# Making the first message table of a four-layer graph network inside the third gather pass

## The chip, the cores and the metric

One core of a Trainium2 chip runs the whole program. The metric is the time of one execution on the device in microseconds. TensorE (PE), VectorE (DVE), ScalarE (ACT), GpSimd (POOL) and SyncE (SP) each run their own instruction list in order and meet at semaphores. All work is in float32.

## What is computed

Four graph layers follow each other over 12,500 nodes of 128 features and 200,000 edges, sorted by destination. The edges stay the same; each layer gathers source rows and sums them by destination. The end of the third layer and the start of the fourth are what matters here:

```
x  = layernorm(x + sage2(relu(sage1(x))))        # third layer, two weighted gathers
h  = x                                            # fourth layer, three steps
for _ in range(3):
    t   = einsum('nd,kod->kno', h, W_et) + b_et   # a row per node and edge type (4 types)
    msg = t[etypes, src]
    a   = segment_sum(msg, dst)
    h   = gru(a, h)
gate = sigmoid(concat([h, x]) @ i_w.T + i_b)
out  = layernorm(x + gate * (h @ j_w.T + j_b))
```

The table `t` of the first step, 12,500 rows of 4 x 128 numbers, must be complete in HBM before the fourth layer's first gather can start.

## The kernel before, in words

Nodes are handled in 25 groups of 512 (`GN`, four tiles `A` of 128). There are six gather passes: pass 1 is the second layer, passes 2 and 3 are the two halves of the third, passes 4 to 6 are the steps of the fourth. A pass walks over 71 turns of four quarters q. In a quarter

- ScalarE copies the source indices of four slots into `stage` (line 1214), once TensorE has summed the same quarter of the turn before (semaphore `summed`), and counts `staged`;
- GpSimd waits for `staged` and issues four indirect DMAs (line 1012), 128 rows each, into `ring`;
- VectorE adds the sum of the turn before to `acc` (line 2007) and builds four one-hot matrices (line 2044, `hot_ready`);
- TensorE, when the rows have landed and the one-hots are there, sums the four slots (line 1566).

Beside that the most used source and destination pairs are summed as dense blocks. SyncE loads them as units from `t_pairs` into two halves of a buffer (lines 652 and 657), VectorE reduces a unit over the types (line 2032) and TensorE multiplies it (line 1549). There are six units in a **step** of two turns. The sixth is left unreduced in passes 2 and 3: TensorE multiplies it straight from the buffer, four matmuls of 128x512 at the end of the step (line 1544), and SyncE may load the second unit of the next step, which takes the same half of the buffer, only after `dense_done` has counted these four.

`pairs_of_turns` (line 448) writes this order out: `body(p)` is the even turn 2p and then the odd turn 2p+1, for p from 0 to 33. Into the quarters of body p the work on one finished group, step p-1, is laid as `parts`. In pass 3, TensorE transposes the group's rows in quarter 0 of the even turn (line 1604) and multiplies in quarter 1 (lines 1625, 1626). ScalarE copies sums and rows in quarter 0 of the odd turn (lines 1248, 1252) and takes the root in quarter 2 (line 1258), for which it waits on VectorE's moments (line 2167). VectorE combines and takes the moments in quarter 1 of the odd turn (lines 2202 to 2167) and writes the normed rows in quarter 3 (line 2179, `step_rows`), which SyncE stores to `t_x` (line 724). There are 33 such steps in the loop, some of them on a dummy group, and three in the tail of the pass: 36 for 25 groups.

After pass 3 there is a stage of its own for the table. For each of the 25 groups SyncE reads the rows back (line 743), TensorE transposes them (line 1364), ScalarE makes two copies, one of them the state `aux` (lines 1267, 1269), TensorE multiplies by the types' weights (line 1640), VectorE adds the bias (line 2233) and SyncE stores (line 738). GpSimd's first gather of pass 4 waits for the last store.

Of the kernel before, what the change touches and what calls it, by code (L numbers as in the profile page):

```python
# [14 lines left out]
P = 128  # L15
# [67 lines left out]
def build(nc, x, src, dst, edge_attr_32, edge_type_4, edge_weight, L0_gnn_W, L0_gnn_b, L1_gnn_u, L1_gnn_W1,  # L83
# [4 lines left out]
    with ctx:  # L88
# [15 lines left out]
        X3 = dram("t_x3", [ROWS, D])  # L104
        TT = [dram(f"t_types{i}", [ROWS, KT * D]) for i in range(2)]
# [78 lines left out]
        t_slot = ring.rearrange("p s f -> p (s f)").rearrange("p (s f) -> p s f", s=4)  # L184
# [10 lines left out]
        dense_sum = work[:, 9 * GN:12 * GN].rearrange("p (s f) -> p s f", s=TILES)  # L195
        own = [work[:, (12 + i) * GN:(13 + i) * GN] for i in range(5)]
# [134 lines left out]
        class Dense:  # L331


            def __init__(self, name, loads, prod=True, norm=True, out_=True):
# [8 lines left out]
                if prod and name != "tt":  # L343
                    self.prod = sem(f"{name}_prod")
                if prod and name not in ("wx", "tt"):
                    self.free = sem(f"{name}_free")
# [22 lines left out]
        p_t = Dense("tt", 0, norm=False, out_=False)  # L369
        p_gate = Dense("value", 1, norm=False, out_=False)  # L370
        p_fin = Dense("fin", 1, prod=False)
        state_rows = [sem(f"state_rows{i}") for i in range(2)]
# [8 lines left out]
        t_prod = [sem(f"t_prod{i}") for i in range(2)]  # L381
        t_rows = [sem(f"t_rows{i}") for i in range(2)]
        t_out = [sem(f"t_out{i}") for i in range(4)]
# [81 lines left out]
        def all_steps(eng):  # L465

            eng.wait_ge(regs_ready, 2)
            return loaded(eng.engine, step_total[0:1, 0:1], 1, STEPS + NG, "the kernel writes one of two numbers",
                          STEPS + TAIL_STEPS)[0]

# [49 lines left out]
        def _(sp):  # L520
# [212 lines left out]
            def t_store(at):  # L733

                for hh in range(2):
                    slot = 2 * at.par + hh
                    sp.wait_ge(t_rows[hh], at.g + 1)
                    sp.dma_start(rows(TT[0], at.g)[:, hh * 2:hh * 2 + 2, :], by_tile(t_slot[:, slot, :], 2)
                                 ).then_inc(t_out[slot], 16)


            def state_in(at):
                sp.dma_start(by_tile(cand[:, at.par, :]), rows(X3, at.g)).then_inc(state_rows[at.par], 16)
            state_in(At(0, 0))

            def t_step(at):
                if not at.last:
                    wait(sp, p_t.turned, at.g)
                    state_in(at.plus(1))
                if not at.first:  # L750
                    t_store(at.plus(-1))
            groups(sp, t_step)
            t_store(LAST)

            for slot in range(4):
                sp.wait_ge(t_out[slot], 16 * (NG // 2 + 1 - slot // 2))
# [36 lines left out]
        def _(pool):  # L793
# [237 lines left out]
            for n in range(3):  # L1031
                if n == 0:
                    for slot in range(4):
                        go(t_out[slot], 16 * (NG // 2 + 1 - slot // 2))
# [8 lines left out]
        def _(act):  # L1043
# [165 lines left out]
            def stage_pass(ph, index, k, parts):  # L1209

                def turn(t, part=None):
                    for q in range(NQ):
                        wait(act, summed, (ph - 1) * PS + last(t, q))
                        act.activation(stage[:, q * K:q * K + K], cols(index, t * U + q * K, K), ACT.Copy).then_inc(staged, 1)  # L1214
                        if part is not None and q in parts:
                            part(q)

                def body(p, units):
                    first = isinstance(p, int) and p == 0
                    turn(p * 2)  # L1220
                    g = None if first else step_of(mybir.EngineType.Activation, p - 1)
                    turn(p * 2 + 1, None if first else lambda q: parts[q](before(total, k, p - 1), g, done_by(ph, p - 1, False), before(total, min(k, 1), p - 1)))
                pairs_of_turns(act, body)
                turn(SURE - 1)
# [8 lines left out]
                def step(m):  # L1233
                    g = step_of(mybir.EngineType.Activation, m)
                    for q in sorted(parts):
                        parts[q](before(total, k, m), g, done_by(ph, m, True), before(total, min(k, 1), m))
# [6 lines left out]
            def rows_turned(features=False):  # L1243

                def part(i, g, done, normed_):
# [9 lines left out]
            def step_root():  # L1255
                def part(i, g, done, normed_):
# [7 lines left out]
            stage_pass(3, meta_src, 2, {0: rows_turned(), 2: step_root()})  # L1264
            def state_step(at):
                act.wait_ge(p_t.turned, at.g + 1)
                act.activation(cols(aux, at.g * GN, GN), bank[at.par][:, :], ACT.Copy)
                wait(act, t_prod[1], at.g - 1)
                act.activation(auxs[:, at.par, :], bank[at.par][:, :], ACT.Copy).then_inc(p_t.copied, 1)
            groups(act, state_step)  # L1270


            def gates(i, g, done, normed_):
# [6 lines left out]
            def new_state(i, g, done, normed_):  # L1280
# [38 lines left out]
        def _(pe):  # L1319
# [23 lines left out]
            def ahead(d, prod, slot=None):  # L1343

                turn_rows(d, At(0, 0), slot)

                def step(at):
                    if not at.last:
                        wait(pe, d.copied, at.g)
                        turn_rows(d, at.plus(1), slot)  # L1350
# [4 lines left out]
            def turn_rows(d, at, slot=None):  # L1355

                if slot is None:
                    d.wait_rows(pe, at)
                    src_ = xin[:, at.i, :]
                else:  # L1360
                    pe.wait_ge(state_rows[at.par], (at.pair + 1) * 16)
                    src_ = slot[:, at.par, :]
                for a in range(A):
                    mm = pe.transpose(bank[at.par][:, a * P:(a + 1) * P], src_[:, a * D:(a + 1) * D], ident[:, :])
# [164 lines left out]
            def gather_pass(ph, k, parts, features=False):  # L1529
# [22 lines left out]
                def turn(t, block=None, part=None):  # L1552
                    for q in range(NQ):
# [16 lines left out]
                        if part is not None and q in parts:  # L1570
                            part(q)

                def body(p, units):
# [6 lines left out]
                    turn(p * 2, block, None if first else  # L1580
                         lambda q: parts[q](before(total, k, p - 1), g, done_by(ph, p - 1, False), before(total, min(k, 1), p - 1)))
                    turn(p * 2 + 1, lambda i: block(TILES + i))
# [9 lines left out]
                def step(m):  # L1592
                    g = step_of(mybir.EngineType.PE, m)
                    for q in sorted(parts):
                        parts[q](before(total, k, m), g, done_by(ph, m, True), before(total, min(k, 1), m))
                tail_steps(pe, total, step)

            def turn_step(per):

                def part(i, g, done, normed_):  # L1600
                    pe.wait_ge(step_in, (i + 1) * 16 if per == 1 else normed_ * 32 + 32)
                    wait(pe, step_free, i)
                    for a in range(A):
# [4 lines left out]
            def l1_prod(i, g, done, normed_):  # L1608
# [11 lines left out]
            def l2_prod(wl, wr):  # L1620

                def part(i, g, done, normed_):
                    pe.wait_ge(step_copied, i + 1)
                    for a in range(A):
# [8 lines left out]
            gather_pass(3, 2, {0: turn_step(2), 1: l2_prod(W_2L, W_2R)})  # L1633

            def types(at):

                for a in range(A):
                    if a % 2 == 0:
                        wait(pe, t_rows[a // 2], at.g)
                    mm = pe.matmul(bank[2 + a][:, :], auxs[:, at.par, a * P:(a + 1) * P],  # L1640
                                   wT[:, W_ET:W_ET + KT, :].rearrange("p k f -> p (k f)"), start=True, stop=True)
                    if a % 2:
                        mm.then_inc(t_prod[a // 2], 1)
            ahead(p_t, types, slot=cand)

            def gate_sums(i, g, done, normed_):
# [675 lines left out]
```

## Time and profile before

| | us |
|---|---|
| median of three runs (15437.32 to 15471.95) | 15470.18 |
| the profiled execution | 15606.01 |
| its span | 15604.3 |
| gathers of pass 3 | 7995 to 9831 |
| tail of pass 3 | 9831 to 9888 |
| the table's own stage | 9888 to 10027 |
| passes 4, 5, 6 | 10027, 11850, 13670 onwards |

The profiled execution is 136 us slower than the median of the runs. Over the span TensorE is busy 64%, GpSimd 62%, VectorE 44%, ScalarE 9%. These are averages over stages with different limits, so they say little about one of them: a stage is to be read by its own rows and by what ends its waits.

### The profile page before, as it was taken

The page shows a single profiled execution, that of the slowest core. Times are in us where ns is not written, and L with a number is a line of the kernel's source. Part 1 is how long each engine was busy: PE and PEld are TensorE (multiplying, and loading weights), DVE is VectorE, ACT ScalarE, POOL GpSimd, SP SyncE. Part 2 cuts the span into 40 slices and gives each one's busy share as a digit, 9 for nine tenths or more (in the row PEclk, how much of TensorE's full clock was granted, in tenths as well). Part 3 has the DMA queues.
Part 4 walks back from the last instruction along what each step waited for, and adds up shares of the span by engine and source line. Part 5 has one row for each costly group of instructions (what it writes and reads, how often), then busy time and mean ns, then how long its engine had stood idle before and what let it go on. Part 6 is the DMA issues. An engine that isn't in the chain of part 4 may idle for free. (4 is left out here: it accounts for less than half of the span.)

```text
span 15604.3 us, 173214 instructions
## 1 busy us (share of the span) xinstructions
PE 10001.7 (64%) x37130; PEld 6386.2 (41%) x37131; DVE 6791.8 (44%) x20397; ACT 1405.0 (9%) x4108; POOL 9688.3 (62%) x8863
## 2 busy tenths in 40 slices
PE   5777774444466666555545555587876888677775
PEld 3444444334344444333333333344443444334443
DVE  3333333333466764666646665333332333222223
ACT  1111111111100000000000000100000000000001
POOL 3888887777646665666655555366664666566662
PEclk6555656667777886667766676799987999788886
DMA  8888887777787774777746666577764777467773
GB/s 271 196 197 197 196 173 152 165 161 122 127 209 189 189 187 117 188 187 189 190 123 175 180 180 164 155 212 203 210 187 137 211 210 208 128 183 190 192 190 84
DMA packets 4070001, 2778.79 MB, mean 178 GB/s; under 512 B 430093, under 2 KB 3820298, under 8 KB 4069630
## 3 DMA queue, kind: packets, MB, share of 16 engines
q1 hardware_dynamic: 3529604, 2147.73, 50.0%
q0 software_dynamic: 508368, 612.97, 20.7%
q10 hardware_dynamic: 31722, 15.04, 0.3%
q14 instruction: 241, 1.97, 0.0%
q8 instruction: 66, 1.08, 0.0%
HBM read 2025.54 MB, written 778.19 MB: 180 GB/s over the span
## 5 line engine op out<-in xcount | busy, mean ns | idle before, releaser
L1012 POOL DMA_INDIRECT ring<-t_types,stage x3408 | 3263.5, 958 | 2275.8 <-issue 1405.0
L1012 POOL DMA_INDIRECT ring<-t_x,stage x2272 | 2207.4, 972 | 1524.4 <-issue 896.7
L1544 PE MATMUL bank<-work 128*128 128x512 f32 x5216 | 2645.9, 652 | 635.1 <-DMA work<-t_types 259.9
L1566 PE MATMUL bank<-ring 128*128 128x128 f32 x13632 | 2285.4, 323 | 1021.1 <-DVE ring L2044 323.9
L1566 PEld LDWEIGHTS bank<-ring 128*128 128x128 f32 x13632 | 2124.4, 232 | 1825.6 <-issue 1574.2
L2032 DVE TENSOR_REDUCE work<-work 128x512 f32<-128x2048 f32 x524 | 1912.1, 3649 | 823.0 <-DMA work<-t_pairs 749.2
L968 POOL DMA_INDIRECT t_sums<-ring,stage x1136 | 1765.3, 1554 | 443.5 <-issue 256.0
L2007 DVE TENSOR_TENSOR acc<-acc,bank 128x128 f32 x1704 | 480.0, 282 | 3513.6 <-remote 2056.2
L1544 PEld LDWEIGHTS bank<-work 128*128 128x128 f32 x5216 | 1041.3, 211 | 1782.5 <-issue 1439.5
L1012 POOL DMA_INDIRECT ring<-t_h,stage x1136 | 1077.7, 949 | 812.9 <-ACT stage L1214 424.7
L1549 PE MATMUL bank<-work 128*128 128x512 f32 x1048 | 734.3, 789 | 547.3 <-issue 320.7
L2044 DVE TENSOR_SCALAR ring<-iota_f,meta_low 128x128 f32<-128x128 f32 x4544 | 999.3, 289 | 1.7 <-issue 1.4
L1443 PE MATMUL bank<-aux 128*128 128x128 f32 x2272 | 527.7, 407 | 571.1 <-ACT aux L1141 535.8
L987 POOL DMA_INDIRECT t_pairs<-acc,pair_stage x432 | 675.6, 1564 | 332.8 <-DMA t_pairs<-acc,pair_stage 192.2
L1910 DVE SCALAR_TENSOR_TENSOR aux<-bank,aux,upto 128x128 f32<-128x128 f32 x1136 | 330.6, 347 | 1182.5 <-PE bank L1428 853.8
L1503 PE MATMUL bank<-aux 128*128 128x128 f32 x864 | 221.4, 437 | 930.5 <-ACT aux L1181 930.5
L1562 PE MATMUL bank<-ring,rec 128*33 128x128 f32 x2272 | 388.4, 324 | 613.3 <-issue 299.7
L1443 PEld LDWEIGHTS bank<-aux 128*128 128x128 f32 x2272 | 468.1, 305 | 704.7 <-ACT aux L1141 597.5
L994 POOL DMA_INDIRECT t_sums<-ring,stage x432 | 672.3, 1556 | 131.6 <-issue 129.5
L2044 DVE TENSOR_SCALAR ring<-iota_f,meta_low,meta_w 128x128 f32<-128x128 f32 x2272 | 653.4, 356 | 147.5 <-issue 145.9
L1562 PEld LDWEIGHTS bank<-ring,rec 128*33 128x33 f32 x2272 | 272.4, 132 | 808.3 <-issue 725.5
L1503 PEld LDWEIGHTS bank<-aux 128*128 128x128 f32 x864 | 189.8, 324 | 959.2 <-ACT aux L1181 958.6
(298 smaller groups left out, 11218.8 us busy)
## 6 DMA issues: line engine op xcount, KB each, us to landing
work<-t_pairs SPq DMA_DIRECT2D x2352, 512.0 KB
t_pairs<-acc SPq DMA_DIRECT2D x272, 740.0 KB
t_pairs<-acc SPq DMA_DIRECT2D x272, 370.0 KB
t_pairs<-acc SPq DMA_DIRECT2D x74, 1360.0 KB
work<-t_types SPq DMA_DIRECT2D x294, 256.0 KB
t_types<-work SPq DMA_DIRECT2D x144, 512.0 KB
ring<-t_types,stage POOLq DMA_INDIRECT x3408
ring<-t_x,stage POOLq DMA_INDIRECT x2272
```

The source lines that it names most:

```text
L968: pool.indirect_dma_start(TAB[k], bass.IndirectOffsetOnAxis(ap=stage[:, u:u + 1], axis=0), msg[:, u, :], None, compute_op=ALU.add).then_in ...
L987: pool.indirect_dma_start(rows_, bass.IndirectOffsetOnAxis(ap=pair_stage[:, u:u + 1], axis=0), pair_out[:, b, k * 2 * P:(k + 1) * 2 * P], ...
L994: pool.indirect_dma_start(TAB[k], bass.IndirectOffsetOnAxis(ap=stage[:, u:u + 1], axis=0), msg[:, u, :], None, compute_op=ALU.add).then_in ...
L1012: pool.indirect_dma_start(msg[:, u, :], None, table, bass.IndirectOffsetOnAxis(ap=stage[:, u:u + 1], axis=0)).then_inc(slot_dma[u], 16)
L1443: mm = pe.matmul(bank[4 + q][:, k * P:(k + 1) * P], dups[:, q, k * P:(k + 1) * P], wx_rows[:, q, :], start=True, stop=True)
L1544: mm = pe.matmul(bank[4 + half][:, :], dense_t[:, tile, k_ * D:(k_ + 1) * D] if ph > 3 else dense_x[:, tile, :], dense_b[:, half, k_ * 4:( ...
L1549: mm = pe.matmul(bank[4 + half][:, :], dense_x[:, tile, :], dense_sum[:, c % TILES, :], start=first, stop=end)
L1562: pe.matmul(bank[q][0:DE + 1, P:2 * P], rec[:, u, 0:DE + 1], hot[:, u, :], start=k_ == 0, stop=k_ == K - 1)
L1566: mm = pe.matmul(bank[q][:, 0:P], msg[:, u, :], hot[:, u, :], start=k_ == 0, stop=k_ == K - 1)
L2007: v.tensor_tensor(into, into, bank[q][:, 0:P], ALU.add).then_inc(added, 1)
L2032: v.tensor_reduce(dense_sum[:, c % TILES, :], dense_b[:, half, :, :].rearrange("p (k b) c -> p (b c) k", k=KT), AXIS.X, ALU.add).then_inc( ...
L2044: ins = v.tensor_scalar(hot[:, q * K + k_, :], iota_f[:, :], low(c + k_), weight(c + k_) if weight else None, ALU.is_equal, ALU.mult if we ...
```

## The change

The stage for the table disappears. Its work is laid into pass 3 as `heads`, per step, 36 times, with the normed rows taken from the tile `s_res` where they were read back from HBM.

- TensorE, in the odd turn of body p, after its sum in the quarter (and after the dense unit): quarter 0 transposes the rows of step p-1, for which it waits on `step_rows`; quarters 1 and 2 each make two tiles of the table, each tile as a one-row matmul that puts the bias in and a 128x512 matmul; quarter 3 makes another product, with the gate's weights.
- ScalarE, in the even turn of body p+1, after its index copies of quarters 1, 2 and 3: the two copies of the transposed rows; tiles 0 and 1; tiles 2 and 3 and then the gate product. Each of these is a wait for TensorE, a wait for the DMA that last left this slot, a copy of 128x512 and a DMA issued on ScalarE's own queue.
- Two slots: `rec` for tiles 0, 2 and the gate product, `b2_all` for tiles 1 and 3.
- A new tensor `t_gate` in HBM takes the gate product; no instruction reads it.
- New waits: TensorE's transposes of the next step and its next products wait for ScalarE's copies (`head_rows`); the norm waits for the transposes of the step before (`head_turned`).
- `pairs_of_turns` writes three bodies out ahead of its loop, before it was two.

```
-            body(0, NH * TILES)
-            body(1, NH * TILES)
-            with turns(eng, 2, LEAD) as p:
+            for p in range(3):
+                body(p, NH * TILES)
+            with turns(eng, 3, LEAD) as p:
...
+            def head_turn(i, m):
+                pe.wait_ge(step_rows, i + 1)
+                for a in range(A):
+                    mm = pe.transpose(bank[6][:, a * P:(a + 1) * P], s_res[:, a * D:(a + 1) * D], ident[:, :])
+                mm.then_inc(head_turned, 1)
+            def head_types(two):
+                def part(i, m):
+                    if two:
+                        pe.wait_ge(head_rows, m * 5 + two)
+                    else:
+                        pe.wait_ge(head_copied, m + 1)
+                    for a in (two, two + 1):
+                        pe.matmul(bank[7 - a % 2][:, :], ones_f[0:1, :], bet_all[0:1, :], start=True, stop=False)
+                        pe.matmul(bank[7 - a % 2][:, :], s_xT[:, a * P:(a + 1) * P],
+                                  wT[:, W_ET:W_ET + KT, :].rearrange("p k f -> p (k f)"), start=False, stop=True).then_inc(head_prod, 1)
+                return part
+            def head_gate(i, m):
+                pe.wait_ge(head_rows, m * 5 + 3)
+                for a in range(A):
+                    mm = pe.matmul(bank[7][:, a * D:(a + 1) * D], s_xT[:, a * P:(a + 1) * P], wT[:, W_I + 1, :], start=True, stop=True)
+                mm.then_inc(head_prod, 1)
+            gather_pass(3, 2, {0: turn_step(2), 1: l2_prod(W_2L, W_2R)},
+                        heads={0: head_turn, 1: head_types(0), 2: head_types(2), 3: head_gate})
...
+            def head_keep(m, a, slot, into):
+                act.wait_ge(head_prod, m * 5 + (a + 1))
+                wait(act, head_out[slot], m * HEAD_OUTS[slot] + a // 2 * 16)
+                act.activation(head_slots[slot], bank[7 - slot][:, :], ACT.Copy).then_inc(head_rows, 1)
+                act.wait_ge(head_rows, m * 5 + (a + 1))
+                act.dma_start(into, by_tile(head_slots[slot], A if a == A else 1)).then_inc(head_out[slot], 16)
...
-            groups(sp, t_step)
-            t_store(LAST)
-            groups(act, state_step)
-            ahead(p_t, types, slot=cand)
-            groups(v, t_add)
```

## Rows read from the trace of the kernel before

**Rows 1.** Windows: pass 3, the table's stage, pass 5, pass 6; columns in its head.

```profile
core 0: us, PE busy (x) PEld busy (x) DVE busy (x) ACT busy (x) POOL busy (x), PEclk, DMA share, GB/s
7995.00:9831.00 1836.00, 936.04 (x3508) 642.51 (x3508) 1125.45 (x2203) 95.37 (x379) 1076.80 (x1136) 0.69 0.65 170
...
9887.80:10027.50 139.70, 105.44 (x300) 47.99 (x300) 68.23 (x118) 27.41 (x54) 0.04 (x1) 0.93 0.74 247
11850.00:13600.00 1750.00, 1363.58 (x4508) 733.62 (x4508) 523.61 (x1743) 117.13 (x380) 1084.61 (x1136) 0.89 0.71 194
13670.00:15370.00 1700.00, 1282.93 (x4228) 698.13 (x4228) 437.03 (x1600) 114.39 (x379) 1089.25 (x1135) 0.86 0.68 179
```

**Rows 2.** Waits in pass 3: who waited for whom, us in total, times, longest.

```profile
POOL ring L1012 <- ACT stage L1214: 424.7, 69, 9.2
...
ACT std L1258 <- DVE mv L2167: 453.1, 33, 16.8
```

**Rows 3.** Timeline of one step of pass 3: start, duration, instruction, [idle before <- releaser].

```profile
9013.84 3.65 DVE L2032 TENSOR_REDUCE work<-work 128x512 f32<-128x2048 f32 x1 [14.87 <-DMA work<-t_pairs]
...
9023.84 3.55 PE L1566 MATMUL bank<-ring 128*128 128x128 f32 x16 [0.40 <-issue]
...
9032.34 0.30 ACT L1258 ACTIVATE std<-mv,eps_col 128x4 f32<-128x4 f32 x1 [15.30 <-DVE mv L2167]
...
9033.54 0.95 POOL L1012 DMA_INDIRECT ring<-t_h,stage  x1 [8.50 <-ACT stage L1214]
...
9038.63 1.11 DVE L2179 TENSOR_SCALAR work<-work,mv,rstd 128x128 f32<-128x128 f32 x4
...
9044.16 5.27 PE L1544 MATMUL bank<-work 128*128 128x512 f32 x8
...
9057.39 0.94 POOL L1012 DMA_INDIRECT ring<-t_h,stage  x1 [0.30 <-issue]
...
9059.79 4.24 SPq L652 DMA_DIRECT2D work<-t_pairs  x4
...
9062.11 0.20 ACT L1214 ACTIVATE stage<-meta_src 128x4 uint32 x1 [17.41 <-remote]
...
9066.01 3.66 DVE L2032 TENSOR_REDUCE work<-work 128x512 f32<-128x2048 f32 x1 [15.62 <-DMA work<-t_pairs]
```

**Rows 4.** Timeline of pass 2: two of its 32 steps, line 1544 and SyncE's next load.

```profile
6680.94 4.17 PE L1544 MATMUL bank<-work 128*128 128x512 f32 x8
...
6699.83 1.00 SPq L652 DMA_DIRECT2D work<-t_pairs  x2
...
7643.79 4.03 PE L1544 MATMUL bank<-work 128*128 128x512 f32 x8
...
7647.68 0.70 SPq L652 DMA_DIRECT2D work<-t_pairs  x1
```

**Rows 5.** Prices by line (min/median/max ns): a one-row matmul, a copy, a DMA issue, landing of 738.

```profile
L1377 PE MATMUL bank<-work,ones_f x50: 587/1056/1217, 70.3 to 241.9; 1*128 1x512 f32 x50
...
L1252 ACT ACTIVATE work<-bank x33: 578/579/580, 8065.1 to 9740.5; 128x512 f32<-128x512 f32 x33
...
L1105 ACTq DMA_DIRECT2D t_wx<-work x25: 378/397/7279, 75.4 to 244.3; - x25
...
DMA to landing us min/median/max: 2.8/3.0/4.7
```

**Rows 6.** Timeline of pass 3's tail, the table's stage and the start of pass 4.

```profile
9870.63 1.11 DVE L2179 TENSOR_SCALAR work<-work,mv,rstd 128x128 f32<-128x128 f32 x4
...
9872.41 1.12 PE L1604 MATMUL bank<-ident,work 128*128 128x128 f32 x4 [6.74 <-DMA work<-t_x]
...
9883.55 1.11 DVE L2179 TENSOR_SCALAR work<-work,mv,rstd 128x128 f32<-128x128 f32 x4
...
10009.54 7.03 PE L1640 MATMUL bank<-wT,work 128*128 128x512 f32 x16
...
10027.46 0.94 POOL L1012 DMA_INDIRECT ring<-t_types,stage  x1 [195.53 <-issue]
```

More of the change, by code:

```diff
@@ L368, in build @@
         gate_link = sem("gate_link")
-        p_t = Dense("tt", 0, norm=False, out_=False)
+        head_turned, head_copied, head_prod, head_rows = (sem(f"head_{n}") for n in ("turned", "copied", "prod", "rows"))
+        head_out = [sem(f"head_out{i}") for i in range(2)]
         p_gate = Dense("value", 1, norm=False, out_=False)
         p_fin = Dense("fin", 1, prod=False)
-        state_rows = [sem(f"state_rows{i}") for i in range(2)]
         gate_prod = sem("gate_prod")
@@ L731, in _ @@
             layer_pass(3, 2, [(s_xin, H1), (s_yin, X2)], H1, X3)
[L733 to L751, printed above, removed]
-            groups(sp, t_step)
-            t_store(LAST)
-            for slot in range(4):
-                sp.wait_ge(t_out[slot], 16 * (NG // 2 + 1 - slot // 2))
+            for slot in range(2):
+                sp.wait_ge(head_out[slot], total * HEAD_OUTS[slot])
             def state_pass(n):
@@ L1032, in _ @@
                 if n == 0:
-                    for slot in range(4):
-                        go(t_out[slot], 16 * (NG // 2 + 1 - slot // 2))
+                    for slot in range(2):
+                        go(head_out[slot], total * HEAD_OUTS[slot])
                 else:
@@ L1207, in _, with stage_pass, turn @@
             total = all_steps(act)
-            def stage_pass(ph, index, k, parts):
-                def turn(t, part=None):
+            def stage_pass(ph, index, k, parts, heads=()):
+                def turn(t, part=None, ahead=None):
                     for q in range(NQ):
@@ L1216, in turn, with head @@
                             part(q)
+                        if ahead is not None and q:
+                            for i in (q - 1,) if q < NQ - 1 else (q - 1, q):
+                                ahead(i)
+                def head(m):
+                    if not heads:
+                        return None
+                    g = step_of(mybir.EngineType.Activation, m)
+                    return lambda q: heads[q](m, g) if q in heads else None
                 def body(p, units):
                     first = isinstance(p, int) and p == 0
-                    turn(p * 2)
+                    turn(p * 2, None, None if isinstance(p, int) and p < 2 else head(p - 2))
                     g = None if first else step_of(mybir.EngineType.Activation, p - 1)
-                    turn(p * 2 + 1, None if first else lambda q: parts[q](before(total, k, p - 1), g, done_by(ph, p - 1, False), before(total, min(k, 1), p - 1)))
+                    turn(p * 2 + 1, None if first else lambda q: parts[q](before(total, k, p - 1), g, done_by(ph, p - 1, False), before(total, min(k, 1), p - 1), p - 1))
                 pairs_of_turns(act, body)
-                turn(SURE - 1)
+                turn(SURE - 1, None, head(STEPS - 1))
                 used = used_turns(mybir.EngineType.Activation)
@@ L1235, in step @@
                     for q in sorted(parts):
[L1236 removed]
+                        parts[q](before(total, k, m), g, done_by(ph, m, True), before(total, min(k, 1), m), m)
+                    for q in sorted(heads):
+                        heads[q](m, g)
                 tail_steps(act, total, step)
@@ L1341, in spread, with ahead @@
                 return mm
-            def ahead(d, prod, slot=None):
-                turn_rows(d, At(0, 0), slot)
+            def ahead(d, prod):
+                turn_rows(d, At(0, 0))
                 def step(at):
@@ L1569, in turn @@
                             block(q - 1)
-                        if part is not None and q in parts:
+                        if part is not None and q in at:
                             part(q)
```

124 lines of the change are left out of this document (58 added, 66 removed).

## The prediction, made before the changed kernel was run

> **What bounds the kernel now.** I read the windows first, to see the price of the stage that goes. The table's stage takes 139.7 us with TensorE busy for 105 of them and no gather under way [rows 1]. That is the most the change can win outside pass 3: 0.9% of the span. So what decides is what pass 3 pays for the work it takes in.
>
> Averages leave room there: in 1836 us TensorE is busy for 936, GpSimd for 1077, ScalarE for 95 [rows 1]. The waits correct this. GpSimd stood 424.7 us for ScalarE's index copies and ScalarE 453.1 us for VectorE's moments, 33 times [rows 2]. So I followed one step through its timeline [rows 3]; all 32 steps of the loop look alike. It is a closed ring:
>
> - VectorE starts on the second dense unit at 9013.84 and works without a pause to the end of the norm at 9038.63 + 1.11 = 9039.74: **25.9 us**.
> - Its moments release ScalarE's root at 9032.34, behind which the next index copy is queued; gathers resume at 9033.54, land, are summed, and line 1544 starts at 9044.16: **4.4 us** after the norm's end.
> - SyncE may load the next step's second unit only after line 1544. By its record that ends at 9049.43, but SyncE issues at 9059.79: **15.6 us** from the start of line 1544.
> - The load lets VectorE start at 9066.01: **6.2 us**.
>
> 25.9 + 4.4 + 15.6 + 6.2 = 52.1; from 9013.84 to 9066.01 it is 52.2. This ring, not an engine's busy share, is the bound of pass 3.
>
> **What is removed.** The stage: 142.8 us from the last norm's end (9884.66) to the first gather of pass 4 at 10027.46 [rows 6]. SyncE's 25 reads and VectorE's 100 adds go with it; they cost nothing beyond it.
>
> **What remains at the end.** Each of the three tail steps gets its head behind its norm, in series: transposes 1.1, two copies 1.2, four tiles at two 128x512 matmuls each (0.88 each by line 1640, eight in 7.03 us [rows 6]; 1.06 by the median of the one-row matmul [rows 5]) with a copy of 0.6 between halves, some 8.5, then the gate product's copy, which waits for the landing of tile 2's DMA because both leave from the same slot: 3.0 [rows 5]. About 15 us to the last copy, then 0.4 to issue and 3.0 to land. Before, the next step's transposes began 0.7 us after a norm (9871.74 to 9872.41 [rows 6]); ScalarE will now be some 12 us later, twice: 24. With 17 to 18 for the last head and some 6 from the last landing to a first gather, 48 remain of 142.8. **The end wins 95 us** (bounds 85 to 103: all matmuls at the low or the high clock).
>
> **What is added to a step of pass 3, 32 times.** TensorE gets four transposes, eight 128x512 matmuls (four of them one row deep, which cost the same [rows 5]) and four small ones: 9 us at the high clock, 17 at the low one. The busy share would carry that. The place is the trouble. Transposing step p-1 stands in quarter 0 of the odd turn and waits for the norm, which VectorE writes in quarter 3 of the same turn. The sums of quarters 0 and 1 now run at 9023.84 to 9027.39 and the norm ends at 9039.74 [rows 3], with VectorE busy all the way. So TensorE stands for about 15 us after its first sum, and everything behind it in its list comes after the norm: transposes 1.1, sum 1.8 (3.55 for two [rows 3]), unit 1.1, two tiles 5.3 (four matmuls, as line 1544 takes here [rows 3]), sum 1.8, unit 1.1, two tiles 5.3, sum 1.8, and only then line 1544. That is 19.3 us where 4.4 stand now; at the high clock 12.7, at the low one 24. ScalarE's copies between the halves lie beside the units. I take **17**, since the granted clock is 0.69 in this pass and 0.89 in pass 5, where TensorE has more to do [rows 1].
>
> Against that, the 15.6 us behind line 1544 can shrink. They aren't matmul time. In pass 2 the same four matmuls release SyncE 3.9 us after their start in one step (7643.79 to 7647.68) and 18.9 in another (6680.94 to 6699.83) [rows 4]. Where it is long, the release comes shortly after GpSimd's last gather (1.5 us after 9058.33 [rows 3]); the trace doesn't say why. Bounds 3.9 and 18.9; with GpSimd running dry earlier in the new step I take **10**, between.
>
> The Trainium skill (Perfetto Trace Analysis, Tensor Engine Instruction) says that a matmul's end in a trace is estimated and that its semaphore moves when PSUM has acknowledged the writes. By that alone the release would follow the records at about 5 us, and the sum below would be 54.1 a step, and in all 34 us faster than now; the trace disagrees here in every step (15.6).
>
> ScalarE gets seven copies of 0.58 and five issues of 0.4 a step [rows 5]: 6 us, in pieces behind index copies; the gate's piece waits 3 us or more for a landing and comes ahead of the odd turn's first index copy. TensorE's line 1544 covers it; without that cover it costs 3 to 5 us a step. VectorE gets nothing; its new wait is long satisfied. SyncE's queue loses nothing in the pass. DMA gets 1.25 MB a step where 8.9 go through now (170 GB/s for 52 us): nothing to 1 us in landing.
>
> **The sum.** 25.9 + 17 + 10 + 6.2 = 59.1 a step against 52.2: 6.9 more, 32 times, 221 us. Less 95 at the end: **126 us slower** than the profiled 15606, 15732. The runs' median lies 136 lower; put on it, 15470 + 125 gives 15595. The break-even is 3.0 us a step: the two uncertain terms (17 and 10) together must stay under 23.
>
> **The rivals.**
>
> - *The ring stays near its length, and the stage's time is won (faster).* Place: between line 1544 and SyncE's load. If the 10 fall to 3.9, the step is 53.0, 0.8 more: 26 less 95, 69 us faster, 15400. With TensorE at the high clock throughout (12.7) it would be 48.7 and 15265. For it: the short release in pass 2 [rows 4], and the clock of 0.89 in pass 5 [rows 1]. It decides from a release under 6 us at 17. Against it: 15.6 in every step of this very pass.
> - *They cancel*: 17 and a release of 5 to 7: 15430 to 15510.
> - *The release stays at 15.6* and the chain is 19.3: 67.0 a step, 14.8 more, 474 less 95: 15850. For it: the release is that long now [rows 3]. The Trainium skill (TensorE: Matmul & The Clock Gate, The HAM clock gate) says that an idle array falls to the half clock and gets the full one back only with sustained work. A stand of 15 us just ahead of the chain would then put it at 19 to 24 and not at 13.
> - *ScalarE's piece with the gate product comes late* by 3 to 5 us in each step: 100 to 160 on top of the forecast, 15700 to 15750.
> - *The change doesn't do what it says*: 36 heads are made for 25 groups and a gate table that nobody reads is stored. That is counted above.
>
> **The numbers.** Forecast, a step longer by 4.5 to 12 us: 0.5. Release and chain at their long ends, or ScalarE late beyond that: 0.12. Cancelled: 0.15. Faster: 0.23. About 0.3% (46 us) is what a measurement of this kernel can tell from no change. So slower 0.62, same 0.15, faster 0.23. The range takes in the cases from most of the faster one to the release at 15.6: 15380 to 15860; the forecast's own is 15520 to 15760.
>
> **What would show it.** In pass 3, the transposes of the head must start right after line 2179's end, with an idle of 12 us or more before them put down to VectorE; line 1544 some 17 us after the norm; a step of 57 to 63 us; GpSimd's wait for ScalarE over 425 us. Pass 4 must start about 48 us after the last norm. I am wrong if TensorE doesn't stand for the norm, if the step stays at 52 or 53 with a release under 6 us, or if passes 4 to 6 change by more than a few us.

## The result, and the profile after

The changed kernel takes **15,703 us** (median of 4 runs, 15,679 to 15,713) where the kernel before takes 15,471 (4 runs): a ratio of **1.0153, 95% interval 1.0137 to 1.0169**, 232 us slower. Forecast were 125 us more, with 0.62 for slower.

First gather to last gather, from the traces, in us:

| | pass 3 | last gather of pass 3 to first of pass 4 | both | the profiled execution |
|---|---|---|---|---|
| before | 1835.6 | 196.5 | 2032.1 | 15,606.0 |
| after | 2125.5 | 124.1 | 2249.6 | 15,703.6 |
| difference | +289.9 | -72.4 | **+217.5** | +97.6 |

The profiled execution of the kernel before stood 136 above its median; in that of the changed kernel every pass that the change doesn't touch is 19 to 27 us shorter, pass 5 for example 1704 against 1725. Set against the medians (+232), the +217.5 of the stretch that was changed is nearly the whole result.

The windows of the changed kernel (core 0): pass 3, the time from the last norm to the first gather of pass 4, and passes 5 and 6 (columns as in [rows 1]).

```profile
7943.00:10070.00 2127.00, 1342.15 (x4432) 765.91 (x4432) 1116.33 (x2202) 227.13 (x610) 1077.41 (x1136) 0.69 0.62 167
10163.10:10193.20 30.10, 18.98 (x28) 6.65 (x28) 14.67 (x19) 4.56 (x11) 0.00 (x0) 0.50 0.32 99
11989.00:13694.00 1705.00, 1361.22 (x4492) 730.58 (x4492) 521.96 (x1731) 116.62 (x379) 1089.69 (x1136) 0.90 0.72 199
13788.00:15468.00 1680.00, 1261.52 (x4228) 689.45 (x4228) 438.13 (x1599) 113.62 (x379) 1092.02 (x1136) 0.87 0.68 181
```

TensorE took in 406 us of work in pass 3 (936 before), and the pass grew by 290: 9.1 us in each of 32 steps. The granted clock stayed at 0.69.

The waits of pass 3 (who waited for whom: us in total, times, longest):

```profile
POOL ring L989 <- ACT stage L1191: 728.3, 155, 8.2
...
ACT std L1247 <- DVE mv L2195: 495.2, 33, 17.9
...
PE bank L1649 <- DVE work L2209: 451.7, 32, 14.8
...
ACT rec L1264 <- DMA t_types<-rec: 5.3, 3, 2.6
```

The third line is the new one: 32 times TensorE stood for the norm (line 2209 now), 14.1 us each. GpSimd's wait for indices rose from 425 [rows 2] to 728. The last line says that ScalarE hardly ever waited for a slot's landing.

One step of the changed kernel from its norm on, to be laid beside [rows 3]: line 2209 is the norm, 1649 the head's transposes, 1569 the sums, 1660 the one-row matmuls of the bias, 1661 the table's matmuls, 1547 the dense unit that SyncE's load (651) waits for.

```profile
9031.92 1.11 DVE L2209 TENSOR_SCALAR work<-work,mv,rstd 128x128 f32<-128x128 f32 x4 [0.22 <-DVE rstd L2202]
...
9033.08 1.11 PE L1649 MATMUL bank<-ident,work 128*128 128x128 f32 x4 [14.00 <-DVE work L2209]
...
9039.48 2.07 PE L1660 MATMUL bank<-bet_all,ones_f 1*128 1x512 f32 x2 [1.87 <-ACT work L1258]
...
9041.48 2.08 PE L1661 MATMUL bank<-wT,work 128*128 128x512 f32 x2
...
9047.36 1.91 PE L1569 MATMUL bank<-ring 128*128 128x128 f32 x8
...
9051.52 1.12 PE L1660 MATMUL bank<-bet_all,ones_f 1*128 1x512 f32 x2 [1.26 <-ACT b_all L1264]
...
9058.23 1.74 PE L1569 MATMUL bank<-ring 128*128 128x128 f32 x8
9059.80 3.60 PE L1547 MATMUL bank<-work 128*128 128x512 f32 x8
...
9063.43 4.28 SPq L651 DMA_DIRECT2D work<-t_pairs  x4
...
9069.86 3.65 DVE L2060 TENSOR_REDUCE work<-work 128x512 f32<-128x2048 f32 x1 [19.05 <-DMA work<-t_pairs]
```

The transposes start 0.05 us after the norm's end (9033.03). From there to line 1547 it is 26.8 us (4.4 before), of which the two halves of the table take 7.9 (9039.48 to 9047.36) and 6.7 (9051.52 to 9058.23). But SyncE is released **3.6 us** after line 1547 starts, where it was 15.6. From the release to VectorE it is 6.4 (6.2 before), and VectorE's part is 25.9, as before.

The granted clock of that chain, in three windows:

```profile
9033.00:9040.00 7.00, 5.05 (x15) 3.45 (x16) 3.10 (x12) 1.26 (x3) 3.67 (x4) 0.50 0.69 182
9040.00:9048.00 8.00, 8.00 (x12) 2.48 (x10) 3.13 (x1) 0.00 (x0) 2.98 (x4) 0.50 0.13 33
9048.00:9059.80 11.80, 10.54 (x24) 4.89 (x24) 1.31 (x5) 1.37 (x3) 3.79 (x4) 0.65 0.20 67
```

0.50 is the level of 1.2 GHz: the first half runs at it from end to end. This is not so in every step: in 17 of the 33 steps of the pass the first half takes 7.9 us, in the others 4.8 to 7.0.

The tail and the start of pass 4, beside [rows 6]:

```profile
10095.76 1.11 DVE L2209 TENSOR_SCALAR work<-work,mv,rstd 128x128 f32<-128x128 f32 x4 [0.21 <-DVE rstd L2202]
...
10129.20 1.11 DVE L2209 TENSOR_SCALAR work<-work,mv,rstd 128x128 f32<-128x128 f32 x4 [0.22 <-DVE rstd L2202]
...
10162.00 1.11 DVE L2209 TENSOR_SCALAR work<-work,mv,rstd 128x128 f32<-128x128 f32 x4 [0.22 <-DVE rstd L2202]
...
10193.32 0.94 POOL L989 DMA_INDIRECT ring<-t_types,stage  x1 [123.17 <-issue]
```

Two tail norms are 33.4 and 32.8 us apart where they were 12.9, and the first gather comes 30.2 us after the last norm's end.

### The profile page after: what moved, and what is told of

Its sections match the earlier page's. It is cut to its first block and busy times, and to the rows that moved or that the text cites. A ratio compares the mean times of both kernels' runs of the same rounds, so it can differ in the third digit from the quotient of the medians.

```text
span 15702.0 us, 174771 instructions
## 1 busy us (share of the span) xinstructions
PE 10338.2 (66%) x37838; PEld 6476.8 (41%) x37839; DVE 6714.4 (43%) x20297; ACT 1520.6 (10%) x4310; POOL 9701.8 (62%) x8863
## 5 line engine op out<-in xcount | busy, mean ns | idle before, releaser
L1547 PE MATMUL bank<-work 128*128 128x512 f32 x5216 | 2615.5, 646 | 586.6 <-DMA work<-t_types 227.1
L1552 PE MATMUL bank<-work 128*128 128x512 f32 x1048 | 721.3, 777 | 366.4 <-issue 240.6
L1446 PEld LDWEIGHTS bank<-aux 128*128 128x128 f32 x2272 | 475.2, 309 | 679.0 <-ACT aux L1118 599.6
L1191 ACT ACTIVATE stage<-meta_src 128x4 uint32 (+1 forms) x852 | 170.8, 203 | 4400.7 <-PE bank L1569 2069.9
```

Source lines behind the costliest of these rows:

```text
L1446: mm = pe.matmul(bank[4 + q][:, k * P:(k + 1) * P], dups[:, q, k * P:(k + 1) * P], wx_rows[:, q, :], start=True, stop=True)
L1547: mm = pe.matmul(bank[4 + half][:, :], dense_t[:, tile, k_ * D:(k_ + 1) * D] if ph > 3 else dense_x[:, tile, :], dense_b[:, half, k_ * 4:( ...
L1552: mm = pe.matmul(bank[4 + half][:, :], dense_x[:, tile, :], dense_sum[:, c % TILES, :], start=first, stop=end)
```

## The experiments

In all of them the kernel before takes **13,798 to 13,815 us**, not 15,471. They ran on three chips (which chip the first runs were on isn't recorded), and the three agree. So I took both kernels' profiles again beside the experiments. "This setting" below is that of these runs, "the first" that of the runs above. Each number below is set against the runs of the kernel before on the same chip; "step" is the median distance of line 1544 (or its successor) in pass 3.

**1. The bias left out** (so the first types' table lacks it): four of each head's eight 128x512 matmuls go.

```
-  pe.matmul(bank[7 - a % 2][:, :], ones_f[0:1, :], bet_all[0:1, :], start=True, stop=False)
   pe.matmul(bank[7 - a % 2][:, :], s_xT[...], wT[...],
-            start=False, stop=True)
+            start=True, stop=True)
```

> Leaves out the bias of the first types' table: the four one-row 128x512 matmuls of each head. Theory (the chain on TensorE from the norm's end to line 1547 sets the step): its two halves of four 128x512 matmuls took 8.0 and 6.9 us and shrink to about 4 each; the chain falls from 26 to 18 or 19 us, the release behind line 1547 stays at 3.9, the step falls from 62.1 to 54 or 55, 7 to 8 us 32 times; with 8 us less in each of three tail steps about 250 us less: 15455, bounds 15420 to 15510. Rival (chain and release share one bound, so that a shorter chain gives a longer release): chain 18, release 8 to 12, step 59 to 62: 15600 to 15690.

Measured: 13,924 us, 1.0092 (1.0075 to 1.0109) of the kernel before. Beside the changed kernel on these chips (14,232, experiment 6) that is 308 less: step 57.8 to 48.8, from the norm to line 1547 21.6 to 12.3, release 3.6. Forecast were 250. The chain theory stands, and nothing came back behind line 1547, though in this setting no kernel shows a long release (experiments 5 and 6). One step's second half:

```profile
8773.23 1.98 PE L1660 MATMUL bank<-wT,work 128*128 128x512 f32 x4 [1.40 <-ACT b_all L1264]
8775.05 1.05 PE L1569 MATMUL bank<-ring 128*128 128x128 f32 x8
8775.94 3.60 PE L1547 MATMUL bank<-work 128*128 128x512 f32 x8
```

Two matmuls in 1.8 us. In the changed kernel four take 6.3 (median): taking half of the work away removed more than two thirds of the time. What is left runs at the full clock: 1.00 in the second halves, where the changed kernel has 0.65.

**2. The gate product left out** (its table isn't read by anything): `heads={..., 3: head_gate}` goes on TensorE and ScalarE, and the counts of five pieces a head become four.

> Leaves out the gate product of each head, its copy and its store (a table that nobody reads). Theory (only what stands between the norm and line 1547 counts in the loop): the gate product stands behind line 1547, so the step stays at 62; only the tail gives back some 2 to 4 us a step: 15670 to 15700. Rival (ScalarE's gate piece comes ahead of the odd turn's first index copy and makes the gathers late by 3 to 5 us a step): 15540 to 15610.

Measured: 14,214 us, 1.0306 (1.0289 to 1.0323): 17 less than the changed kernel, most of it in the pass (8 us) and the tail (4). The rival with ScalarE's piece, 100 to 160 us in my prediction, falls.

**3. No wait for the norm.** The transposes read s_acc in place of s_res, so the table holds other values, and wait for the combining adds alone:

```
-  pe.wait_ge(step_rows, i + 1)
+  pe.wait_ge(step_free, i + 1)
-  ... pe.transpose(bank[6][...], s_res[...], ident[:, :])
+  ... pe.transpose(bank[6][...], s_acc[...], ident[:, :])
```

> The head's transposes read s_acc in place of s_res (the table's values are other ones), so TensorE waits in quarter 0 only for the combining adds (which end near 9030 in the step of rows 3) and not for the norm (9039.7); all the work stays. Theory (the stand for the norm is what lengthens the step): line 1547 comes about 26 us after the adds and not after the norm, some 9 us earlier; step 52 to 54: 15370 to 15460. Rival 1 (the work itself, at the low clock, costs it): step 60 to 62, 15640 to 15700. Rival 2 (the long release behind line 1547 comes back when TensorE is early): line 1547 earlier, release 12 to 16, step 59 to 62: 15600 to 15700.

Measured: 13,939 us, 1.0099 (1.0082 to 1.0116), so 293 less than the changed kernel with all of its work kept. TensorE still stood, for the adds:

```profile
PE bank L1649 <- DVEq L2249: 166.2, 32, 5.9
```

5.2 us each in place of 14. Line 1547 came some 13 us after the norm, step 49.6, release 4.2. The place of the wait, not the work, costs two thirds of the 434 us. Rival 2 (a long release coming back) can't be judged here, since no trace of this setting has one.

**4. The wait alone**, on the kernel before: nothing is moved, TensorE only waits for the norm in quarter 0.

```
-  turn(p * 2 + 1, lambda i: block(TILES + i))
+  turn(p * 2 + 1, lambda i: block(TILES + i), None if first or ph != 3 else
+       lambda q: pe.wait_ge(step_rows, before(total, k, p - 1) + 1) if q == 0 else None)
```

> The kernel before, with nothing moved, and one wait more: in pass 3 TensorE waits in quarter 0 of the odd turn for the norm of the step before, as the head's transposes do. Theory A (a stand of TensorE ends the long release behind line 1544): two units and three sums now follow the norm, line 1544 starts 8 to 9 us after it and not 4.4, the release falls from 15.6 to 4 or 5, the ring would be 45 and the step 45 to 50 us: 15220 to 15400. Theory B (the release is a thing of its own, or of GpSimd's stream, and stays near 15.6 or falls only by what the chain grew): step 52 to 56.5, 15470 to 15610.

Measured: 13,845 us, 1.0031 (1.0019 to 1.0044). One step:

```profile
8618.69 1.11 DVE L2180 TENSOR_SCALAR work<-work,mv,rstd 128x128 f32<-128x128 f32 x4
8620.15 2.04 PE L1566 MATMUL bank<-ring 128*128 128x128 f32 x8 [13.79 <-DVE work L2180]
...
8629.65 4.23 SPq L652 DMA_DIRECT2D work<-t_pairs  x4
```

(The norm is line 2180 in this kernel.) Line 1544 starts at 8626.02, 6.2 after the norm's end, and the release is 3.6. 25.9 + 7.2 + 3.6 + 6.5 = 43.2, and the step is 43.2: the ring adds up to the tenth. A stand of 14 us costs 45 us in all, when only three sums and two units are behind it. In pass 3 alone the wait costs 44 us (experiment 4), the work with a shorter wait 243 (experiment 3), and both together 509 (experiment 6): most of the price is that the work stands behind the wait. But neither theory on the release could be judged here, as the next two runs show.

**5 and 6. Both kernels again, unchanged.**

> The kernel before, unchanged, for its profile: the runs of the first four experiments, with the kernel before among them, took 13800 us where it took 15470 at first, and in their traces the release behind line 1544 or 1547 is 3.6 to 3.9 in pass 2 and 3 alike. Expected: the kernel before shows it too where it takes 13800: a release of about 3.6 in place of 15.6, and a step of pass 3 of 40 to 42 (25.9 + 4.4 + 3.6 + 6.5 = 40.4; 32 gathers at 1.25 are 40.0). Rival: its release stays near 15.6 and it is the changed kernels that lost it.

> The changed kernel, unchanged. If the chain alone sets the step where the release is short: 25.9 + 21 to 24 + 3.8 + 6.5 = 57 to 61 a step against 40 to 42 before, 18 us 32 times, less 70 to 90 at the end: 430 to 540 us slower than the kernel before on the same chip (14230 to 14340 where that takes 13800). Where the kernel before shows its long release: 230 us slower, as in the first runs. Rival: the change costs the same 230 us everywhere.

Measured: 13,804 us for the kernel before, and 14,232 for the changed one, 1.0316 (1.0299 to 1.0333): **434 us slower** than the 13,798 of all runs of the kernel before in that comparison. The two windows of the kernel before, passes 2 and 3:

```profile
5945.00:7366.00 1421.00, 859.97 (x3508) 589.93 (x3508) 1026.04 (x1773) 93.05 (x346) 1074.68 (x1135) 0.75 0.82 213
7422.00:8890.00 1468.00, 895.55 (x3508) 607.09 (x3508) 1114.83 (x2202) 98.07 (x379) 1079.82 (x1135) 0.71 0.82 212
```

1468 where [rows 1] have 1836, with the engines busy for nearly the same time (TensorE 896 for 936, GpSimd 1080 for 1077). Here is one release of it, line 1544 and SyncE, with GpSimd's gathers running on past it:

```profile
8551.08 4.41 PE L1544 MATMUL bank<-work 128*128 128x512 f32 x8
...
8555.53 4.12 SPq L652 DMA_DIRECT2D work<-t_pairs  x4
8555.86 0.94 POOL L1012 DMA_INDIRECT ring<-t_h,stage  x1 [0.30 <-issue]
```

4.4 us. Counted over all 32 steps of a pass, from the start of line 1544 or 1547 to SyncE's issue of the second unit's load, the one that waits for it:

| trace | pass 2: median, over 6 us | pass 3: median, over 6 us |
|---|---|---|
| before, first | 9.9, 31 of 32 | 15.9, 32 of 32 |
| after, first | 15.9, 31 of 32 | **3.9, 1 of 32** |
| before, again | 4.2, none | 4.6, none |
| after, again | 4.5, none | 3.8, none |

The short release of pass 2 in [rows 4] is not one. SyncE's issue at 7647.68 is the first unit's load (line 657, the rows that come with a first unit, follows it), and the second unit's came at 7653.23, 9.4 us after line 1544's start. The one short release of that pass is at 6344.45:

```profile
7647.68 4.92 SPq L652 DMA_DIRECT2D work<-t_pairs  x2
7652.70 0.35 SPq L657 DMA_DIRECT2D work<-t_x  x1
7653.23 7.83 SPq L652 DMA_DIRECT2D work<-t_pairs  x4
```

```profile
6344.45 3.60 PE L1544 MATMUL bank<-work 128*128 128x512 f32 x8
...
6348.08 8.82 SPq L652 DMA_DIRECT2D work<-t_pairs  x4
```

The long release belongs to the first runs, in both kernels, and no other trace has it. It is not line 1544's alone either. In [rows 3] ScalarE's index copy at 9062.11 comes as late: by its record the sum that it waits for had ended at 9050.32. Counted over the six passes of the kernel before, ScalarE was free and its index copy still came more than 5 us after the end of the sum that it waits for in 338 of 1680 cases in the first trace, at least 41 in each pass, and in none in the second. In the changed kernel's first trace it is 310, but 6 in pass 3. And all six passes of the kernel before are 269 to 367 us longer in its first trace than in its second.

In the changed kernel's first trace it is gone from pass 3, the one pass in which TensorE stands for the norm, and there in pass 2 of the same execution:

```profile
7071.01 4.64 PE L1547 MATMUL bank<-work 128*128 128x512 f32 x8
7087.80 4.10 SPq L651 DMA_DIRECT2D work<-t_pairs  x4
```

Where it doesn't exist, the change can't take it away, and costs 434 us in place of 232. The ring, median of its terms in pass 3:

| | VectorE | norm to 1544/1547 | release | landing | step |
|---|---|---|---|---|---|
| before, first | 25.9 | 4.2 | 15.9 | 6.2 | 52.3 |
| after, first | 25.9 | 25.0 | 3.9 | 6.4 | 62.1 |
| before, again | 25.9 | 4.3 | 4.6 | 6.5 | 41.4 |
| after, again | 26.0 | 21.6 | 3.8 | 6.6 | 57.8 |

Pass 3 is 1978 us for 1469, and from its last gather to the first of pass 4 it is 124.0 for 195.4: +509 - 71 = +437, the measured 434.

**7. The wait alone, a second time**, since it would tell the two theories apart where the long release occurs:

> The kernel before with the one wait more, a second time, for the case that the kernel before takes 15470 in these runs and not 13800: there the release behind line 1544 was 15.6 in pass 3 in every step, and 3.9 in pass 3 of the changed kernel, which is the only pass of that trace in which TensorE stands for VectorE. Theory A (the stand is what ends it): release 4 in pass 3 and 10 to 16 in the other passes, pass 3 about 250 us shorter than with the kernel before. Theory B (it is the amount of work on TensorE, or chance): 15 in pass 3 too. Where the kernel before takes 13800, as in the other runs: +45 us as before, release 3.6, and the question stays open.

Measured: 13,865 us, 1.0034 (1.0014 to 1.0054), release 3.6. The kernel before took 13,815 beside it: 50 us, as before, and the question stays open.

**8. Work in the stand.** Added to the changed kernel, with results that are overwritten:

```
+  pe.wait_ge(step_free, i + 1)
+  for a in range(5):
+      pe.matmul(bank[7][:, :], ident[:, :], wT[:, W_ET:W_ET + KT, :]..., start=True, stop=True)
   pe.wait_ge(step_rows, i + 1)
```

> The changed kernel with work added for the experiment: while TensorE stands for the norm it waits for the combining adds alone at first (they end some 9 us earlier) and then runs five 128x512 matmuls into bank 7, whose results are overwritten, before it waits for the norm. Theory (the stand puts TensorE to the low clock, and that makes the halves behind the norm cost 7 to 8 us each and not 5): the granted clock from the norm to line 1547 rises from 0.5 to 0.65 towards 1.0, the chain falls from 21.4 to 14 to 18 us, the step from 57.8 to 50 to 55: 90 to 240 us less than the changed kernel, 13990 to 14140 where that takes 14231. Rival (nine us of activity don't raise the clock, or the five matmuls overrun the norm by 1 to 3 us): chain 21 to 24, 14230 to 14320.

Measured: 14,225 us, 1.0302 (1.0285 to 1.0319), and step 58.0: no gain. Two windows of one step from the norm's end (8947.4) on, and two of the changed kernel's (8931.7) below them:

```profile
8947.40:8952.50 5.10, 4.52 (x19) 2.17 (x19) 3.32 (x11) 1.26 (x3) 3.88 (x5) 1.00 0.90 242
8952.50:8966.00 13.50, 12.10 (x23) 4.74 (x23) 4.27 (x6) 1.38 (x3) 6.42 (x7) 0.66 0.27 78
```

```profile
8931.70:8941.00 9.30, 9.30 (x23) 4.67 (x24) 6.31 (x11) 1.26 (x3) 6.57 (x7) 0.68 0.58 155
8941.00:8953.20 12.20, 11.10 (x28) 5.60 (x26) 1.32 (x5) 1.37 (x3) 3.79 (x4) 0.64 0.22 70
```

The five matmuls did what was hoped right behind the norm: the clock is 1.00, and the head's transposes, sum and unit took 3.0 us in place of 4.5 (medians). Then it fell, in the midst of the halves, and these took 5.0 and 6.9 in place of 4.8 and 6.3: the chain went from 21.6 to 20.9 and not to 14 to 18. The low stretch was moved, not removed, and my theory that the stand by itself makes the halves dear falls in that form.

**9. The heads behind line 1547** (without the gate product). The transposes go to quarter 3 of the odd turn, behind the dense unit; the halves to quarters 0 and 1 of the next even turn; the step's own transposes and product to quarters 2 and 3 of it. ScalarE's copies follow, and its root waits in quarter 3.

```
+  def both(q):                      # TensorE, even turn
+      if not (isinstance(p, int) and p < 2):
+          ahead_types(q, p)         # heads[q + 1] of step p - 2, for q < 2
+      if q > 1:
+          parts[q - 2](...)
+  turn(p * 2 + 1, ..., lambda q: heads[0](before(total, k, p - 1), p - 1), (NQ - 1,))
```

> The changed kernel without the gate product, and with its heads moved behind line 1547: the transposes in quarter 3 of the odd turn, the two halves in quarters 0 and 1 of the next even turn, the step's own transposes and product in quarters 2 and 3; ScalarE's copies follow, and its root waits in quarter 3 and not 2. Theory (the stand for the norm and the halves between norm and line 1547 cost the step): the transposes find the norm done, line 1547 comes 2 to 5 us after the norm; the step is 40 to 48 where the release is short (TensorE is then busy for 37 to 46 of it): -30 to +130 us against the kernel before; where the release is long, 50 to 54: -100 to +40. Rival (TensorE's 16 us of work itself is too much in a step): 55 to 60, as the changed kernel.

Measured: 13,683 us, **0.9915 (0.9899 to 0.9932), 114 us faster than the kernel before** and 548 faster than the changed kernel. One step, with the norm (2236), the dense unit (1560) and the head (1676, 1687, 1688):

```profile
8421.72 1.11 DVE L2236 TENSOR_SCALAR work<-work,mv,rstd 128x128 f32<-128x128 f32 x4 [0.24 <-DVE rstd L2229]
...
8424.13 3.60 PE L1560 MATMUL bank<-work 128*128 128x512 f32 x8
...
8427.57 0.60 PE L1676 MATMUL bank<-ident,work 128*128 128x128 f32 x4
8427.76 4.51 SPq L651 DMA_DIRECT2D work<-t_pairs  x4
...
8429.43 1.12 PE L1687 MATMUL bank<-bet_all,ones_f 1*128 1x512 f32 x2 [0.37 <-ACT work L1271]
...
8430.48 1.12 PE L1688 MATMUL bank<-wT,work 128*128 128x512 f32 x2
...
8434.76 1.13 PE L1582 MATMUL bank<-ring 128*128 128x128 f32 x8 [1.05 <-DMA ring<-t_h,stage]
```

The transposes wait for nothing, line 1560 comes 1.3 us after the norm (median 1.1), and the first half takes 4.3 us (8429.43 to 8433.72). The pass is 1433 us, and 1136 gathers at 1.25 us, their distance where GpSimd waits for nothing, need 1420: GpSimd's gathers nearly fill it now. Its window has TensorE busy for 1093 us at a clock of 0.83 (0.71 in the changed kernel):

```profile
7415.00:8848.00 1433.00, 1093.23 (x4168) 647.70 (x4168) 1123.44 (x2202) 213.55 (x577) 1081.47 (x1135) 0.83 0.90 242
```

**10. The same with the gate product**, in quarter 2 of the even turn ahead of the step's own transposes, so all that the change added.

> As the kernel with the heads behind line 1547 (13683 us beside 13798 of the kernel before), but with the gate product, its copy and its store as in the changed kernel, in quarter 2 of the even turn ahead of the step's own transposes: all of the work that the changed kernel added. Theory (the gate product has its place beside other work): 0 to 30 us more, 13680 to 13720. Rival (TensorE's list is full at the place, or ScalarE's piece makes an index copy late): 60 to 150 more, 13740 to 13840.

Measured: 13,726 us, 0.9940 (0.9923 to 0.9957), 79 us faster than the kernel before; 42 more than without (36 if each is set against the kernel before on its own chip), between the two expectations. Pass 3 is 1460, so at that place the gate product is not hidden.

**11. The root one quarter later**, alone, on the kernel before: `stage_pass(3, ..., {0: rows_turned(), 3: step_root()})`.

> The kernel before with one edit: in pass 3 ScalarE takes the root of the step's variances behind its index copy of quarter 3 in place of quarter 2, so that the copy doesn't queue behind the wait for VectorE's moments. Theory: gathers no longer pause there, line 1544 follows the norm closer by 0 to 4 us; where the release is short the step is held at 40 by GpSimd's gathers: 0 to -60 us; where it is long: 0 to -180. Rival (the root is later and with it the norm): +0 to +60.

Measured: 13,755 us, 0.9970 (0.9960 to 0.9980): 43 less. Pass 3 is 1428 for 1469, and GpSimd's wait for indices fell from 66.3 to 23.3 us:

```profile
POOL ring L1012 <- ACT stage L1214: 66.3, 78, 4.2
```

```profile
POOL ring L1012 <- ACT stage L1214: 23.3, 71, 1.9
```

So 43 of the 114 us of experiment 9 are to be had without moving the table at all. The other 71 are the stage's: the end gives 75 (195.4 to 120.5), and pass 3 is 1433 there and 1428 here. With the gate product (experiment 10) 36 of the 79 are left beyond these 43.

## Why the prediction was right in sign and short in size

- **The stand for the norm: right.** Forecast about 15 us ahead of the transposes, "right after line 2179's end"; measured 14.1, 0.05 us after it. Experiments 3, 4 and 9 show it as the cause, together with the work behind it: the same work with a shorter wait costs 293 us less, the wait without the work costs 45, and behind line 1547 the heads without the gate product cost 5 us in the pass (1433 for 1428), with it 32.
- **Norm to line 1547: too small, the term that was mis-sized.** I took 17 "since the granted clock is 0.69 in this pass", with 24 as the upper bound. Measured 25.0, above the bound. The pass's mean was the wrong number: the halves had 0.62 on average (0.50 all through the first half of the step shown) and took 7.9 and 6.7 us (medians), not 5.3 each as line 1544 does. What I also left out is ScalarE: 1.3 us of wait for line 1264 between the halves, which I held to lie beside the units, and 42.5 us in 27 steps for line 1258 ahead of the first. Even at the better clock of the later runs (0.86 in the first half) the chain is 21.6, of which 19.3 is my own row-by-row sum; most of the other 2.3 are that wait and slower halves. I should have kept the 19.3 as a floor. The Trainium skill's rule (TensorE: Matmul & The Clock Gate, The HAM clock gate) that an idle array falls to the half clock, which I had only with a rival, agrees with the traces: 0.56 and 0.52 on average in the 14 us of the stand, in the first and the later one. Behind it the two differ, 0.59 and 0.73 in the 15 us after the norm, and no run shows why.
- **The release: too large.** I took 10, with 3.9 and 18.9 as bounds; measured 3.9 (1 of 32 over 6 us). Chain and release together are 28.9 where I had 27 and where the kernel before had 20.1. The lower bound rested on a misread row (the 3.9 us of pass 2 are the first unit's load, experiments 5 and 6): 31 of the 32 releases of that pass were long too, so that the rows spoke less for a short release than I wrote, and that it came is luck. The two misses nearly cancelled: 62.1 a step and not 59.1, 290 us and not 221. That the forecast was near is luck in that sense, since its two terms were each off by 6 to 8 us.
- **What the long release is: open.** It is not a property of the kernel: both kernels show none of it in the later runs. Where it occurs, ScalarE's index copies come late with it, in passes 4 to 6 too, so the ring of pass 3 names only one of its places. A stand of TensorE went with its end in one trace, in 31 steps of 32, but GpSimd stands longer there too, and no edit ran where it occurs. My rival in which "the release stays at 15.6" leaned on its being in every step of pass 3; the faster rival leaned on its falling to 3.9, which it did, but with the chain at 17 or less, which it wasn't.
- **The Trainium skill's rule of the release** (Perfetto Trace Analysis, Tensor Engine Instruction: a semaphore moves when PSUM has acknowledged the writes) would put it at about 5 us. I set it aside against 15.6 in every step; every later trace has 3.6 to 5.8, beside it.
- **The end: 72 won, not 95.** A tail step grew by 20.5 us and not by 12, and the last head took 30.2 from the norm to the gather and not 24. Both are the half clock: the clock is 0.50 in the 30 us after the last norm, and each pair of 128x512 records takes 2.0 us there. (The line on what would show it, "48 us after the last norm", mixed this with the tail steps' delay; by its own working it should have said 24.) The bounds, 85 to 103, were meant to hold all matmuls at either clock; but 1.06 us [rows 5] is the price of one record at the low clock, and a matmul shows as two: 2.0 us.
- **ScalarE late with the gate product: wrong**, 17 us in all (experiment 2), with 3 waits of at most 2.6 us for a landing.
- **36 heads and a table that nobody reads: counted, and small.**
- **Passes 4 to 6: not changed.** They differ by 21 to 26 us between the first two traces and by 3 or less between the two taken side by side.

## What to carry to other kernels

Work moved into a loop goes where its operand is ready and nothing late stands behind it on that engine. Here the busy share had room for all of it (TensorE 936 of 1836 us). The same heads, without the gate product in both places, cost 414 us ahead of the dense unit (experiment 2) and win 71 behind it, beyond what the root's move gives. Follow the ring of the loop through both places before you choose one. A wait for a late result puts all that is queued behind it on that engine behind that result. The stand itself is cheap if little follows: 14 us of it cost 45 us in 32 steps with three sums and two units behind it, and 434 with the heads there. And price matmuls that follow a stand from rows at the low clock, never with the mean of the pass.

## What the runs showed of the hardware

- The same program took 15,471 us in its first runs and 13,798 to 13,815 beside every experiment, with TensorE, VectorE and GpSimd busy in pass 3 for times equal to 5%. What differs in the traces is when waits for a semaphore end. In the kernel before, SyncE's load comes up to 18.9 us after line 1544's start, over 6 us in 63 of 64 steps of passes 2 and 3, and each time GpSimd's stream of gathers has just run dry (SyncE at most 4.3 us behind the last gather, the next one 3.1 us or more behind it); in the later trace it takes 3.6 to 5.8 us with gathers running on. ScalarE's index copies are late in the same way in all six passes. Whether GpSimd's stream is cause or effect, and what differs between the settings, is open. The change cost 232 us in the one setting and 434 in the other.
- Activity put into a stand gave 1.00 for the 5 us right behind it in the step shown (0.68 in the 9 us of the changed kernel), and the clock then fell (0.66 in the next 13.5 us), so nothing was won: 14,225 us for 14,232.
- A 128x512 f32 matmul shows as two records, of 0.59 us at the full clock and 1.06 to 1.2 at half.
